# New slot numbers for the last phase of a two-layer decoder kernel on Trainium2

## The reference

```
x = x + _L1_xattn_ref(_layernorm(x), ctx_768, Wq, Wk, Wv, Wo)   # 16 heads of 16, softmax over 256 context tokens
x = x + _L1_ffn_ref(_layernorm(x), w_gate, w_up, w_down)

def fp4_quant_dequant(x):                 # blocks of 16 along the last axis
    scale = max(|block|) / 6, at least 1e-12
    return grid_value(x / scale) * scale  # grid 0, .5, 1, 1.5, 2, 3, 4, 6
gate, y = fp4_linear(x, w_gate), fp4_linear(x, w_up)   # 256 -> 704
return fp4_linear(silu(gate) * y, w_down)              # 704 -> 256
```

## Time and profile before

| | |
|---|---|
| median of three runs | 3676.26 us (3671.95 to 3680.55) |
| the profiled execution itself | 3674.73 us, with a span of 3673.0 us |
| PE, matmul | 3190.3 us busy, 87% of the span |
| DVE | 2443.8 us, 67% |
| ACT | 1771.3 us, 48% |
| POOL | 1193.8 us, 33% |
| last phase | from about 2271 us to the end |
| TensorE clock granted, mean | 0.961 |

### The profile page before, as it was taken

How to read it: one execution, slowest core, us unless ns; L and a number is a source line. 1 busy time by engine, 2 the same in 40 slices (tenths; PEclk the granted TensorE clock), 3 DMA queues, 4 the chain that set the end, 5 groups by cost and what they waited for, 6 DMA issues and landing times. The chain is left out here.

```text
span 3673.0 us, 57604 instructions
## 1 busy us (share of the span) xinstructions
PE 3190.3 (87%) x21302; PEld 2143.6 (58%) x21302; DVE 2443.8 (67%) x4877; ACT 1771.3 (48%) x3179; POOL 1193.8 (33%) x1868
## 2 busy tenths in 40 slices
PE   4788888888888888869999787789999999999996
PEld 2455555555555555446666555466666666666664
DVE  4588888887788887624211176577777777777774
ACT  3666666666666666311111032344554454545442
POOL 3344444444444444210000153123333332333222
PEclk8899999999999999879999999799999999999998
DMA  4866666666666666333333243434433433443330
GB/s 91 144 96 92 92 92 92 92 92 92 92 91 91 91 90 85 43 109 114 120 122 110 87 146 113 56 48 66 60 52 57 66 57 52 59 69 52 51 45 12
DMA packets 291101, 301.17 MB, mean 82 GB/s; under 512 B 35242, under 2 KB 278426, under 8 KB 290820
## 3 DMA queue, kind: packets, MB, share of 16 engines
q1 hardware_dynamic: 276420, 273.41, 44.9%
q0 software_dynamic: 6144, 15.68, 1.4%
q10 hardware_dynamic: 8256, 8.39, 0.7%
HBM read 95.51 MB, written 50.40 MB: 40 GB/s over the span
## 5 line engine op out<-in xcount | busy, mean ns | idle before, releaser
L492 DVE TENSOR_REDUCE xa_mx<-bank 128x2 f32<-128x512 f32 x1024 | 659.5, 686 | 234.7 <-PE bank L482 233.2
L596 ACT ACTIVATE xa_p<-bank 128x512 f32<-128x512 f32 x1024 | 577.6, 596 | 443.7 <-PE bank L586 440.9
L607 DVE SCALAR_TENSOR_TENSOR xa_p<-xa_p,bank 128x1024 f32<-128x1024 f32 x256 | 311.4, 1217 | 71.3 <-PE bank L575 49.6
L619 PE MATMUL bank<-xa_p,xa_v 128*32 128x256 f32 x4096 | 279.2, 391 | 18.6 <-DVE xa_p L607 18.6
L920 ACT ACTIVATE xa_p<-bank 128x384 f32<-128x384 f32 x512 | 231.7, 493 | 120.8 <-PE bank L908 72.2
L586 PE MATMUL bank<-xa_qs,xa_ks 99*128 99x256 bf16 x1024 | 196.0, 285 | 96.3 <-DMA xa_qs<-xa_row 38.3
L586 PE MATMUL bank<-ex_w,xa_ks 99*128 99x256 bf16 x1024 | 191.9, 280 | 72.3 <-ACT xa_p L596 37.9
L1935 POOL DMA_INDIRECT sa_y<-expert_out,sa_s x64 | 70.7, 1105 | 509.7 <-POOLq L1836 483.6
L1749 PE MATMUL bank<-ex_w,ex_h 128*128 128x256 f32 x1024 | 223.9, 379 | 1.0 <-issue 0.9
L1719 PE MATMUL bank<-ex_xt,ex_w 128*128 128x512 f32 x512 | 224.2, 596 | 0.7 <-ACT ex_xt L1710 0.7
L1730 ACT ACTIVATE ex_h<-bank,ex_b 128x512 f32<-128x512 f32 x64 | 44.0, 687 | 361.3 <-PE bank L1719 361.3
(11 more groups left out here) (282 smaller groups left out, 6806.3 us busy)
## 6 DMA issues: line engine op xcount, KB each, us to landing
ex_w<-ra_parts SPq DMA_DIRECT2D x384, 128.0 KB, 5.3
xa_ks<-xa_pk SPq DMA_DIRECT2D x384, 128.0 KB, 4.6
ex_w<-in_L_ffn_W SPq DMA_DIRECT2D x32, 1024.0 KB, 7.1
xa_qs<-xa_pq SPq DMA_DIRECT2D x192, 128.0 KB, 5.7
ex_w<-xa_pq SPq DMA_DIRECT2D x192, 128.0 KB, 6.7
ra_x<-in_x SPq DMA_DIRECT2D x32, 256.0 KB
xa_ctx<-in_ctx_t SPq DMA_DIRECT2D x64, 128.0 KB, 4.3
queue<-zeros ACTq DMA_DIRECT2D x4, 2048.0 KB, 8.1
```

The source lines that it names most:

```text
L492: c.nc.vector.tensor_reduce(c.xa.row_max[:, :, n], halves(c.banks[2 + n % 2]), AX.X, ALU.max).then_inc(s.max_taken, 1)
L596: c.nc.scalar.activation(c.xa.p_beside[:, n // 2 % 4, :, n % 2, :], halves(c.banks[n % 2]), ACT.Exp, scale=SCALE).then_inc(s.exp, 1)
L607: c.nc.vector.scalar_tensor_tensor(out=p, in0=p, scalar=1.0, in1=c.banks[bank][:, :].unsqueeze(1).broadcast_to([P, TC, 2 * S]), op0=ALU.mi ...
L619: m = c.nc.tensor.matmul(bank[WIDE * quad:WIDE * quad + WIDE, at + q0:at + S], v[:, kc, 4 * g + quad, :], p(4 * g + quad, kc), start=(kc = ...
```

## The change

Only the numbers in the five tables change (and the count of slots, so that all fit). No piece is added, removed or changed in itself, no semaphore, no buffer and no bank. What differs is the order in each engine's queue. The period stays 80 slots. A few lines stand for all:

```
-LAST_E = (B - 1) * SLOTS_E + 580
+LAST_E = (B - 1) * SLOTS_E + 1325
...
-        for b, k in due(n, SLOTS_E, 221, 9, 4):
+        for b, k in due(n, SLOTS_E, 1093, 8, 4):
             pe_xa_sum(c, c.xa.s.exp, 16 * (B + b) + 4 * k + 4, B + b, k)
...
-        for b, k in due(n, SLOTS_E, 346, 10, 4):
+        for b, k in due(n, SLOTS_E, 1184, 19, 4):
             dve_e_hidden(c, b, k)
```

More of the change, by code:

```diff
@@ L2405, in act_phase_e @@
     for n in range(LAST_E):
[L2406 removed]
+        for b, k in due(n, SLOTS_E, 997, 1, H):
             act_xa_exp(c, B + b, k)
[L2408 removed]
+        for b, _ in due(n, SLOTS_E, 846):
             act_xa_high_k(c, 7, c.wx, B + b)
[L2410 removed]
+        for b, _ in due(n, SLOTS_E, 859):
             act_xa_xn_t(c, 6, B + b)
[L2412 removed]
+        for b, _ in due(n, SLOTS_E, 853):
             act_xa_middle_k(c, B + b)
[L2414 removed]
+        for b, _ in due(n, SLOTS_E, 878):
             act_xa_high_q(c, 6, c.wx, B + b)
[L2416 removed]
+        for b, _ in due(n, SLOTS_E, 899):
             act_xa_middle_q(c, B + b)
[L2418 removed]
+        for b, _ in due(n, SLOTS_E, 881):
             act_xa_values(c, 7, B + b)
[L2420 removed]
+        for b, _ in due(n, SLOTS_E, 1009):
             act_xa_raw(c, B + b, 0)
[L2422 removed]
+        for b, _ in due(n, SLOTS_E, 1015):
             act_xa_raw(c, B + b, 1)
[L2424 removed]
+        for b, _ in due(n, SLOTS_E, 1034):
             act_xa_out_t(c, B + b)
[L2426 removed]
+        for b, _ in due(n, SLOTS_E, 1088):
             act_e_xn_t(c, 6, b)
[L2428 removed]
+        for b, _ in due(n, SLOTS_E, 959):
             act_xa_rows(c, 2, 1, B + b)
[L2430 removed]
+        for b, k in due(n, SLOTS_E, 1092, 3, 4):
             act_e_silu(c, b, k)
[L2432 removed]
+        for b, k in due(n, SLOTS_E, 1211, 9, 3):
             act_e_hid_t(c, 2 + k % 2, b, k)
@@ L2437, in pool_phase_e @@
     for n in range(LAST_E):
-        for b, _ in due(n, SLOTS_E, 56):
+        for b, _ in due(n, SLOTS_E, 0):
             pool_xa_power(c, B + b)
-        for b, _ in due(n, SLOTS_E, 106):
+        for b, _ in due(n, SLOTS_E, 0):
             pool_xa_low_k(c, B + b)
-        for b, _ in due(n, SLOTS_E, 132):
+        for b, _ in due(n, SLOTS_E, 2):
             pool_xa_low_q(c, B + b)
-        for b, _ in due(n, SLOTS_E, 165):
+        for b, _ in due(n, SLOTS_E, 80):
             pool_xa_split_max(c, B + b)
-        for b, _ in due(n, SLOTS_E, 285):
+        for b, _ in due(n, SLOTS_E, 162):
             pool_e_power(c, b)
-        for b, _ in due(n, SLOTS_E, 299):
+        for b, _ in due(n, SLOTS_E, 162):
             pool_e_normed(c, b)
-        for b, _ in due(n, SLOTS_E, 382):
+        for b, _ in due(n, SLOTS_E, 251):
             pool_e_quantise(c, b)
@@ L2456, in sp_phase_e @@
     for n in range(LAST_E):
-        for b, _ in due(n, SLOTS_E, 4):
+        for b, _ in due(n, SLOTS_E, 3):
             sp_e_load(c, x_rows[b], b)
-        for b, _ in due(n, SLOTS_E, 4):
+        for b, _ in due(n, SLOTS_E, 0):
             sp_xa_context(c, d["ctx_t"][b], B + b)
-        for b, _ in due(n, SLOTS_E, 130):
+        for b, _ in due(n, SLOTS_E, 6):
             sp_xa_stack_k(c, B + b)
-        for b, _ in due(n, SLOTS_E, 139):
+        for b, _ in due(n, SLOTS_E, 85):
             sp_xa_stack_q(c, B + b)
-        for b, _ in due(n, SLOTS_E, 207):
+        for b, _ in due(n, SLOTS_E, 164):
             sp_xa_max_rows(c, B + b)
-        for b, _ in due(n, SLOTS_E, 579):
+        for b, _ in due(n, SLOTS_E, 530):
             sp_e_out(c, out_rows[b], b)
```

64 lines of the change are left out of this document (28 added, 36 removed).

## The result

The changed kernel takes 3585.39 us, median of four runs (3584.73 to 3587.39), against 3674.11 (3668.39 to 3680.55) for the kernel before. The ratio is 0.9759, with a 95% interval of 0.9741 to 0.9777. A ratio is always to the kernel before, measured beside the kernel in question. The forecast of 3591 lies 5.6 us above what was measured, and the measured time lies inside both ranges. The profiled execution of the changed kernel took 3584.73 us, with a span of 3583.0.

What follows compares the result with a forecast made beforehand. The last phase was taken to hang on PE, but not wholly, with 4.0 us of waits in each 40.62 us period. From 3674.7: -65 for 27 periods, -12 filling, -6 draining gave 3591 us, range 3574 to 3612 (whole range 3572 to 3640).

Steps and rivals of the forecast that it cites:

- The step from which the gain comes: Steady period of the last phase: PE's waits shrink, period 40.62 to 38.2 us, a gain of 2.42 us a period.
- The DVE chain: DVE from the add over both quantisations to its first maximum, freeing the third maximum's bank at 20.3 to 21.1 us.
- short version: Two instructions of line 2210 on DVE take 0.8 us without POOL beside them; bank free at 20.3 us.
- the long one: Line 2210 on DVE keeps 1.56 us for two; bank free at 21.1 us, PE 0.6 late.
- the walk: One period of the new order counted from the projection's start with old distances between starts; it gave 38.2 us.
- rival 1: DVE chain governs, POOL still stretching line 2210 or another step: period 38.7, 3605 us; chance 0.17.
- The port: Port pair shared by POOL and DVE: POOL's last quantisation steps could lengthen the DVE chain by up to about 1 us.
- the prediction's 3606: Time expected near 3606 us if the port rule lengthened the DVE chain by up to about 1 us a period.
- The margins: Projection's bank about 0.3 us in hand, down's copies about 0.2, the maxima's DMA 1.5; costed at nothing.
- Filling: Start of the last phase, before the first down: -12 us, between 0 and -20, SP's new order costing some 2.
- The wait of 5.36 us in the earlier trace: In filling, old order: a product stood behind the small quantisation; the new order puts the products first.
- Draining: End of the last phase: four shorter periods at 1.5 us each, -6 us, between 0 and -10.

Runs made afterwards that it cites:

- e11: Kernel before, with POOL's low part of the queries moved ahead of the second layer norm's power (slot 132 to 124): 3673.28 us, ratio 1.000.
- e2: Changed kernel plus an unused DVE reduction over 704 columns each period, directly ahead of the big quantisation: 3599.29 us.
- e1: Changed kernel with PE's down product back ahead of head 0's score and the last up piece: 3796.36 us, ratio 1.033.
- e4: Changed kernel with POOL's table of before: 3845.22 us, ratio 1.0461.
- e12: Changed kernel with SP's table of before, its six numbers put back: 3598.62 us, ratio 0.9788.
- e5: Changed kernel with the next element's statistics in DVE's idle stretch and SP's loads ahead of the keys' stack: 3589.60 us, ratio 0.9772.
- e10: e7 with DVE's normed tensor for the keys' element two slots earlier, ahead of maxima 10 and 11: 3611.48 us, ratio 0.9832.
- e6: Changed kernel with down cut into four pieces and the scores of heads 1 to 3 between them: 3590.75 us, ratio 0.9775.
- e7: e6 with PE's maxima four slots later (first slot 1025 to 1029): 3641.93 us.

## Why the prediction was right, and where its sizes were off

**The step from which the gain comes** held to 0.2 us at every point. From the projection's start: head 0's score at 3.79 (forecast 3.79), down at 5.19 (5.20), its end at 10.37 (10.38), the third maximum at 20.46 (20.5), and from there 17.81 (17.6). The period is 38.27 where I took 38.2; 27 periods gave 63.3 us for 65. Of 38.27 us, 1.6 are still not PE's own work, and 1.3 of them lie in the five scores (2.48 us for five instead of 1.15). The prediction charged these to the new order ("Now five scores stand in a row"), but the old one pays nearly the same, so they are in both periods.

**The DVE chain** was counted to end at 19.5 by the short version of line 2210 and 20.3 by the long one, and the first maximum starts at 19.59. The short version was right, and e11 shows its cause. That the sum came within 0.1 is in part luck: the big quantisation starts 11.43 us after the projection where the walk has 11.64, and the 0.24 that line 1513 lost made up for it. How near the choice was is an estimate from e2: had line 2210 kept its 0.83 us more, POOL's last steps would have come later with it, so line 1513 would have kept its 0.24, and beyond the slack of 0.13 PE would have paid 0.70 a period. That is a period of 38.97 and 19 us in all, where rival 1 had 38.7 and 14 (3605 against 3591).

**The port.** POOL's L1536 ends at 2933.72, line 1513 starts at 2933.33 and ends at 2933.78, and takes 0.45 us instead of 0.21. The step waited for POOL's to end; it lost 0.24 us a period, since only the end of POOL's step fell on it, and since PE doesn't wait at the third maximum this costs nothing. The price of up to 1 us is seen once, in the first element, where POOL's L1536 began 0.07 us ahead (2395.30 to 2396.36):

```profile
2395.37 1.05 DVE L1513 TENSOR_SCALAR fp_s<-fp_s 128x88 f32<-128x88 f32 x1
```

This is the rule of the Trainium skill that stood against the change (SBUF — State Buffer, "SBUF: two separate sides": the pair of ports is an exclusive lock, and the loser is blocked), and here the trace agrees. It does not in e11: there POOL's L284 (2923.15 to 2923.99, 128x2) lies beside both L2210 (2923.22 to 2923.95) and stretches neither, and so it is at 58 of the 64 instructions of that line. By the rule as the page has it, any GpSimd operation that starts first holds the pair. The measurement decides, though a span on POOL is rough. The sum behind the prediction's 3606 was off too: 1 us more on 20.3 makes a period of 38.9 and 3610 us.

**The margins.** Those I named as thin held: no wait for the projection's bank, none for down's copies, none for the maxima's DMA. The one at the third maximum is 0.13, and I had 0.2. e1 and e4 show what it costs when the cover of a piece or the margin of the DMA is gone: 123 and 172 us slower than the kernel before.

**Filling** was mis-sized: -12 forecast, -16.8 measured, inside its own range. I charged SP's new order with 2 us; by e12 it brings 10. The rest of the filling is then worth 6.7 us and not the 14 of the sum, so the total came as near as it did because two misses cancel. The loads for the second element are indeed late (the second keys wait 6.09 us for their context), but the queries' stack no longer stands behind the keys' stack, and each element of the filling needs it at once. I had looked only at how late the second element's loads come. The wait of 5.36 us in the earlier trace rows did go, and a wait of 3.77 us for DVE's maxima stands at the same place (2403.24 above), so that term was worth less than I took. The granted clock in the filling is 0.87 for 0.82, which I had not counted; how much of the gain is the clock isn't told apart.

**Draining** missed by the most. It was -6, between 0 and -10, and is -13.4: the distances are 35.3, 30.3, 23.8 and 23.7 where they were 39.7, 33.5, 26.5 and 24.8, and the last 1.9 us are won behind the last down. The first is 4.4 shorter, not 1.5. I took 1.5 for each, less than a full period's 2.35, but the gain there is larger. The clock is higher there too (0.93 for 0.89); how much is the clock and how much the order isn't told apart.

The misses add up: +1.7 for the periods, -4.8 for the filling, -7.4 for the draining and +3.4 for the later start are -7.1 us, which brings 3591.7 (the sum as it was made) to 3584.6, and the profiled execution is 3584.7. So the total of 3591 is nearer than its parts: the gain at the two ends was 30.2 us where the sum had 18. The range has a slip as well. With a period of 38.7 and nothing won at either end its upper end would be 3623; the 3612 belongs to a period of 38.3.

## What to carry to other kernels

In a software pipeline of in-order queues, add up the distances between starts for one engine and see which bank or semaphore each piece needs: this walk gave the period to 0.1 us. The durations of the profile hold the latency at the end (0.38 us for a pair that takes 0.23), and a sum of those would not have. When two paths meet at one instruction, find the slack there before shortening either; here it was 0.13 us, and six edits around that place (e5 to e10) brought nothing or lost up to 57 us. Read the filling and the draining by themselves: an order of DMAs that has slack in the steady state can be worth 10 us where every element waits for its first data.

## What the runs showed of the hardware

Waits on PE can cost more than their length. In e1, 2.38 us of idle time were followed by 4 us at a granted clock of 0.57, and the gate piece at 2912.76 in them took 1.70 us instead of 1.18. The mean over 2600 to 3200 us was 0.95, where the changed kernel has 1.00 with 0.67 us of told idle time a period. The long wait is not the only place: over 2944 to 2948 us the clock is 0.57 as well, behind waits of 0.62 and 0.47 us. And e6 and e7, with one wait of 1.26 and of 1.43 us in each period, have 1.00 over 2600 to 3200 us.

In this kernel a VectorE step of [128 x 256] float32 waits for a GpSimd step of 512 columns that began before it: 1.24 us instead of 0.41. The row of before that shows it has the count, then shortest, middle and longest in ns, for the two in one period:

```profile
L2210 DVE TENSOR_SCALAR fe_xn<-sa_x,fe_mv,fe_rstd x2: 401/821/1241, 2926.8 to 2927.9; 128x256 f32<-128x256 f32 x2
```

The first starts at 2926.79 and ends 0.15 us after POOL's L422 (2926.72 to 2927.88); the second, at 2927.9, takes its usual time. The prediction had said that the second was the stretched one.
